# A four-layer attention and feed-forward kernel: the last layer's weights quantised in the second attention's last group, and its rows scaled on ScalarE

## The chip, the core and the metric

The kernel runs on one core of one Trainium2 chip. Such a core has TensorE (PE: matrix products and transposes by a product with the identity, with results in PSUM), VectorE (DVE), ScalarE (ACT), GpSimd (POOL) and SyncE (SP, which here only issues transfers). Each engine runs its own instruction stream; they meet through semaphores. The metric is the device time of one execution in microseconds, median of three runs.

## The reference, cut to what matters

```python
x = x + L0_xattn(layernorm(x), ctx)      # 16 heads of 64
x = x + L0_ffn(layernorm(x))             # top 2 of 8 experts
x = x + L1_xattn(layernorm(x), ctx)      # 16 heads of 16
x = x + L1_ffn(layernorm(x))

def quantize_w8_per(w, axis):            # per row or column
    amax = clip(max(abs(w), axis=axis, keepdims=True), 1e-08, None)
    scale = 127.0 / amax
    return clip(round(w * scale), -128.0, 127.0) / scale
def quantize_a16(x):                     # one scale for the whole tensor
    amax = clip(max(abs(x)), 1e-08, None)
    scale = 32767.0 / amax
    return clip(round(x * scale), -32768.0, 32767.0) / scale
def L1_ffn(x, W_in, b_in, W_out, b_out):
    hidden = gelu(quantize_a16(x) @ quantize_w8_per(W_in, axis=0) + b_in)
    return quantize_a16(hidden) @ quantize_w8_per(W_out, axis=1) + b_out
```

x is 8 batches of 512 rows of 256, W_in is 256x1024, W_out 1024x256, all float32. Because the activations have one scale, nothing of x can be quantised before the largest normalised value of all eight batches is known, and nothing of hidden before the largest of all hidden values.

## The kernel before, in words

The four layers run one after another, each in blocks in which every engine has its own stream and at whose end all engines meet. A batch is 512 rows, as QT = 4 tiles of 128 rows on the partitions. x stays in SBUF as `x_sb` from the experts to the end of the second attention and is also stored, batch by batch, to `x_between` in HBM, from which the last layer loads it.

**The second attention** (`second_attention`, L1200) goes through 8 batches of four groups of four heads. While PE and ScalarE work on the scores and exponentials of one group (`scores` L1498, `exps` L1657, `probs_v` L1505), PE computes the maximum scores of the next group and VectorE reduces them (`take_max`, L1754). In the very last group there is no next group, so VectorE's `attend` (L1776 and around) only keeps and divides the output of the group before (`keep_o` L1769, `divide`), and then waits for the last `keep_o`. After that come the transposes of the outputs (L1592), the output projection (L1612), the addition to x (L1826) and the store of the batch (L1411). On SP's queue the load of the input weights, `spare<-in_winT` (L1409), stands ahead of that store, as soon as `spare`, which the attention uses for its normalised rows, is free.

**The last layer** (`quantised_layer`, L1892) has five blocks; the change touches the first and the third.

1. Normalisation. SP loads the eight batches of x (`f_hid<-x_between`, L2012 for batches 0 and 1, each with its own semaphore, L2015 for 2 to 7, with one semaphore between them), two biases, and, when PE has turned the input weights and left `spare`, the output weights into `spare` (L2021). VectorE first quantises the input weights (`quantise_weights`, L1903: the largest magnitude of each row, 127 over it, eight scalings by row tile with a rounding constant added, one subtraction of it). PE turns them (L2031) and ScalarE copies them to `win`. Then for each batch VectorE takes the statistics (`row_statistics`: four `bn_stats` L67, four `bn_aggr` L73, variance plus epsilon L76), GpSimd raises that to the power -0.5 (L2095), VectorE subtracts the mean and multiplies (`scale_rows`, L84: four tiles) and reduces the largest magnitude (L2070), PE turns the batch (L2042: eight transposes) and ScalarE copies it to `xnT` (L2053). The statistics run one batch ahead; batches 2 to 6 are in a loop of two batches.
2. `whole_amax`: the maximum over partitions, through PE (L1962 to L1978).
3. First projection. For each batch VectorE rounds the rows (L2122), ScalarE makes the high part (L2177), VectorE the low part (L2128), PE multiplies both by `win` (L2168: 32 products), ScalarE applies gelu (L2183) and VectorE reduces the largest magnitude (L2135). After the first two batches' low parts VectorE quantises the output weights from `spare` into `wout` (the same L1903 to L1923).
4. `whole_amax` again, and 5. the second projection (L2252 to L2349) with the residual from `x_between`, the bias on GpSimd (L2332) and the store.

The order of every engine's work is written out by hand; there is no planner.

Of the kernel before, what the change touches and what calls it, by code (L numbers as in the profile page):

```python
# [13 lines left out]
P = 128  # L14
# [1185 lines left out]
def second_attention(nc, x_sb, ident, ident_r, mhalf, d, ctx_parts, x_dram, spare, s_win, s_xs):  # L1200


    with ExitStack() as ctx:
# [152 lines left out]
        def _(sp):  # L1356
# [38 lines left out]
            def batch(b, left):  # L1395
# [343 lines left out]
        def _(dve):  # L1739
# [59 lines left out]

            def keep_v(b, t):  # L1800
# [91 lines left out]
def quantised_layer(nc, ident, ones, mhalf, d, x_dram, out, spare, s_win, s_xs):  # L1892
# [5 lines left out]
    with ExitStack() as ctx:  # L1898
# [3 lines left out]
        def quantise_weights(dve, w, whole, top, s, inv, loaded, need, s_wq):  # L1902


            dve.wait_ge(loaded, need)
            nc.vector.tensor_reduce(top[:], w[:], AX.X, ALU.max, apply_absolute_value=True
                                    ).then_inc(s_wq, 1)
            dve.wait_ge(s_wq, 1)
            nc.vector.tensor_scalar(top[:], top[:], TINY, None, ALU.max).then_inc(s_wq, 1)
            dve.wait_ge(s_wq, 2)  # L1910
            nc.vector.reciprocal(s[:], top[:]).then_inc(s_wq, 1)
            dve.wait_ge(s_wq, 3)
            nc.vector.tensor_scalar(s[:], s[:], 127.0, None, ALU.mult).then_inc(s_wq, 1)
            dve.wait_ge(s_wq, 4)
            nc.vector.reciprocal(inv[:], s[:]).then_inc(s_wq, 1)

            for t in range(FFT):
                nc.vector.tensor_scalar(w[:, t, :], w[:, t, :], s[:, t:t + 1], MAGIC,
                                        ALU.mult, ALU.add).then_inc(s_wq, 1)
            flat = w[:].rearrange("p t k -> p (t k)")  # L1920
            whole = whole[:].rearrange("p t k -> p (t k)")
            dve.wait_ge(s_wq, 13)
            nc.vector.tensor_scalar(whole, flat, MAGIC, None, ALU.subtract).then_inc(s_wq, 1)  # L1923

# [7 lines left out]
        wout = sb("wout", [P, FFT, D], F32R)  # L1932
        bin_ = sb("b_in", [P, FFT])
        bout = sb("b_out", [P, D])
        win_max = sb("win_max", [P, FFT])
        win_s = sb("win_s", [P, FFT])
# [43 lines left out]
        with ExitStack() as ab:  # L1980
# [4 lines left out]
            with ExitStack() as a:  # L1985
# [20 lines left out]
                with nc.Block() as block:  # L2006
# [49 lines left out]
                    def _(dve):  # L2056
# [393 lines left out]
```

## Time and profile before

| | us |
|---|---|
| median of 3 runs (3283.21 to 3284.38) | 3283.84 |
| the profiled execution | 3282.52 |
| its span | 3280.7 |
| PE busy | 3100.5 (95%) |
| VectorE busy | 2288.7 (70%) |
| ScalarE busy | 1630.7 (50%) |
| GpSimd busy | 1304.9 (40%) |

The span is what the profile's records cover; some 1.8 us of the profiled execution lie around it. Times in the rows below count from its start. Busy shares are averages over the whole run; the last layer starts near 3058.9 and has other limits than the attentions that fill the rest. [...]

### The profile page before, as it was taken

How to read it: one execution, taken by the hardware profiler on the slowest of the kernel's cores; microseconds unless marked ns; L12 is line 12 of the kernel's file. 1: busy time of each engine (PE TensorE's matmuls, PEld its weight loads, DVE VectorE, ACT ScalarE, POOL GpSimd, SP SyncE). 2: the span in 40 equal slices, each digit the busy share in tenths (PEclk: the TensorE clock that was granted, in tenths of full speed). 3: DMA queues.
4: the chain of work that ended last, by engine and by line, in shares of the span. 5: the costliest groups of instructions: out<-in, count | busy, mean ns of one | idle time of the engine just before them, and what ended most of it. 6: DMA issues, size and time to landing. Idle time of an engine off the chain costs nothing. (4 is left out here: it accounts for less than half of the span.)

```text
span 3280.7 us, 40332 instructions
## 1 busy us (share of the span) xinstructions
PE 3100.5 (95%) x14204; PEld 1883.9 (57%) x14204; DVE 2288.7 (70%) x3680; ACT 1630.7 (50%) x1850; POOL 1304.9 (40%) x610
## 2 busy tenths in 40 slices
PE   6999999999999999999999969799999999999588
PEld 4556556556566565565565446455555555554368
DVE  5775775665766757757747434788888888888589
ACT  3453443443444434534534412376576666666388
POOL 1774774764765756747647723200000000000102
PEclk8999999999999999999999989799999999999698
DMA  8444553463453444444435232322323223322202
GB/s 233 113 117 120 127 139 90 117 158 85 117 145 90 119 125 118 107 122 113 120 100 124 65 113 73 83 49 64 71 49 69 66 49 72 67 50 57 72 13 90
DMA packets 182474, 317.40 MB, mean 97 GB/s; under 512 B 35080, under 2 KB 94288, under 8 KB 182288
## 3 DMA queue, kind: packets, MB, share of 16 engines
q1 hardware_dynamic: 182288, 315.00, 38.6%
q8 instruction: 107, 1.75, 0.2%
q14 instruction: 79, 0.65, 0.1%
HBM read 92.58 MB, written 29.36 MB: 37 GB/s over the span
## 5 line engine op out<-in xcount | busy, mean ns | idle before, releaser
L907 POOL TENSOR_TENSOR a_prob_sum<-a_prob_sum,a_prob 128x1024 f32<-128x1024 f32 x384 | 918.3, 2391 | 57.1 <-ACT a_prob L623 1.8
L623 ACT ACTIVATE a_prob<-a_t 128x1024 f32<-128x1024 f32 x512 | 517.0, 1025 | 647.9 <-PE a_t L442 461.9
L770 DVE TENSOR_REDUCE a_mhalves<-a_m 128x1 f32<-128x512 f32 x1024 | 688.6, 680 | 106.9 <-PE a_m L406 98.4
L1657 ACT ACTIVATE a_prob<-a_t 128x1024 f32<-128x1024 f32 x512 | 497.4, 1025 | 183.4 <-PE a_t L1498 182.7
L1754 DVE TENSOR_REDUCE a_mhalves<-a_m 128x1 f32<-128x512 f32 x807 | 537.2, 685 | 61.5 <-PE a_m L1477 57.5
L449 PE MATMUL a_o<-a_prob,a_v_all 128*64 128x512 f32 x2048 | 493.7, 604 | 0.0
L406 PE MATMUL a_m<-a_kh_n,a_qz 128*128 128x512 f32 x1024 | 416.9, 419 | 10.3 <-DVE a_kl_n L764 5.8
L907 POOL TENSOR_TENSOR a_prob_sum<-a_prob 128x1024 f32<-128x1024 f32 x64 | 153.5, 2398 | 557.5 <-ACT a_prob L623 494.3
L1477 PE MATMUL a_m<-a_vh,a_qz 128*128 128x512 f32 x807 | 337.1, 438 | 10.2 <-DVE x_sb L1826 4.4
L434 PE MATMUL a_t<-a_q_hl,a_k_hh 128*128 128x512 f32 x1024 | 325.1, 398 | 0.3 <-ACT a_prob L623 0.3
L442 PE MATMUL a_t<-a_q_hm,a_k_lm 66*128 66x512 f32 x1024 | 320.9, 394 | 0.0
L1498 PE MATMUL a_t<-a_qs,a_vs 128*128 128x512 f32 x1024 | 318.6, 400 | 1.6 <-ACT a_qs L1676 0.9
L406 PEld LDWEIGHTS a_m<-a_kh_n,a_qz 128*128 128x128 f32 x1024 | 187.4, 188 | 205.0 <-issue 95.7
L1868 POOL TENSOR_TENSOR a_rstd<-a_veps,mhalf 128x4 f32<-128x4 f32 x8 | 8.1, 1018 | 718.1 <-DVE a_veps L76 718.1
L786 DVE RECIPROCAL a_recip<-a_x 128x128 f32<-128x128 f32 x256 | 239.3, 944 | 48.5 <-PE a_x L465 48.5
L1505 PE MATMUL a_o<-a_prob,a_v_all 128*18 128x512 f32 x2048 | 269.7, 598 | 0.4 <-ACT a_prob L1657 0.4
L1477 PEld LDWEIGHTS a_m<-a_vh,a_qz 128*128 128x128 f32 x807 | 152.5, 190 | 191.4 <-DVE a_mhalves L1754 127.7
L449 PEld LDWEIGHTS a_o<-a_prob,a_v_all 128*64 128x64 f32 x2048 | 125.0, 136 | 223.7 <-issue 193.5
L761 DVE TENSOR_TENSOR a_ql_n<-a_x,a_qz 64x512 fp32r<-64x512 f32 x128 | 88.1, 689 | 227.4 <-ACT a_qz L639 225.2
L442 PEld LDWEIGHTS a_t<-a_q_hm,a_k_lm 66*128 66x128 f32 x1024 | 193.4, 189 | 43.5
L1498 PEld LDWEIGHTS a_t<-a_qs,a_vs 128*128 128x128 f32 x1024 | 184.9, 188 | 58.1 <-ACT a_prob L1657 17.1
L434 PEld LDWEIGHTS a_t<-a_q_hl,a_k_hh 128*128 128x128 f32 x1024 | 188.3, 189 | 50.3 <-ACT a_prob L623 11.1
(273 smaller groups left out, 4187.2 us busy)
## 6 DMA issues: line engine op xcount, KB each, us to landing
a_k_hh<-a_kh_n SPq DMA_DIRECT2D x256, 256.0 KB, 4.2
a_k_lm<-a_kl_n SPq DMA_DIRECT2D x128, 256.0 KB, 4.8
a_q_hl<-a_qz SPq DMA_DIRECT2D x128, 128.0 KB, 2.3
a_q_hm<-a_qz SPq DMA_DIRECT2D x128, 128.0 KB, 2.4
a_q_hl<-a_ql_n SPq DMA_DIRECT2D x128, 128.0 KB, 2.3
a_vs<-a_vh SPq DMA_DIRECT2D x256, 64.0 KB, 2.4
a_wq<-wq_parts SPq DMA_DIRECT2D x63, 256.0 KB, 2.6
a_wk<-wk_parts SPq DMA_DIRECT2D x63, 256.0 KB, 2.9
```

The source lines that it names most:

```text
L406: pe.matmul(ps_m[:, n, :], qz[:, hd, qt * P:(qt + 1) * P], kh_n[:, n * 512:(n + 1) * 512], start=True, stop=True).then_inc(s_mx, 1)
L434: pe.matmul(ps_t[t % 2][:, hd, :], k_hh[:, u, hd, keys], q_hl[:, u, hd, :], start=True, stop=False)
L442: mm = pe.matmul(ps_t[t % 2][:, hd, :], k_lm[0:HD0 + 2, u, hd, keys], q_hm[0:HD0 + 2, u, hd, :], start=False, stop=True)
L449: mm = pe.matmul(ps_o[hd * HD0:(hd + 1) * HD0, :], v_all[:, t, (2 * pr.p + hd) * HD0:(2 * pr.p + hd + 1) * HD0], prob[:, t % RING, hd, :], ...
L623: nc.scalar.activation(prob[:, t % RING], ps_t[t % 2][:, :, :], ACT.Exp, scale=SCALE0).then_inc(s_exp, 1)
L770: nc.vector.tensor_reduce(mhalves[:, qt, hd, n:n + 1], ps_m[:, n, :], AX.X, ALU.max).then_inc(s_max, 1)
L907: nc.gpsimd.tensor_tensor(acc, prob[:, (t - 1) % RING] if t == 1 else acc, prob[:, t % RING], ALU.add).then_inc(s_acc, 1)
L1477: pe.matmul(out, qz[:, u, h, qt * P:(qt + 1) * P], vh[:, G // 2 % 2, k * 512:(k + 1) * 512], start=True, stop=True).then_inc(s_mx, 1)
L1498: mm = pe.matmul(ps_t[j][:, h, :], vs[:, u, 2 * j + h, keys], qs[:, u, 2 * j + h, :], start=True, stop=True)
L1505: mm = pe.matmul(ps_o[QD * h:QD * h + VW, :], v_all[:, t, GH * n + h, :], prob[:, t % RB, h, :], start=(t == 0), stop=(t == KT - 1))
L1657: nc.scalar.activation(prob[:, t % RB, 2 * j:2 * j + 2, :], ps_t[j][:, :, :], ACT.Exp, scale=SCALE1).then_inc(s_exp, 1)
L1754: nc.vector.tensor_reduce(mhalfs[:, u, qt, h, k:k + 1], bank, AX.X, ALU.max).then_inc(s_max, 1)
```

## The change

- The output weights get their own tile `wout` and a half-size tile `raw`, allocated ahead of the experts. SP loads the input weights as before, then the first half of the output weights into `raw`, waits until VectorE has quantised it, and loads the second half; only then comes the wait and store of the last batch.
- In the second attention's last group VectorE, after `divide`, quantises the first half, the input weights, and the second half (`quantise_weights`, now a function of its own, for a range of row tiles). Both calls in the last layer are gone, and so is the load of the output weights there.
- In the normalisation block rows are scaled on ScalarE: rstd times x plus a shift, where the shift, minus the mean times rstd, is one VectorE operation of 128x4 for a batch. VectorE's order for a batch is now statistics two batches ahead, the largest magnitude, the shift two batches ahead. ScalarE scales batch b+1 before it copies batch b.
- All loops of that block are written out. GpSimd waits until ScalarE has read the rstd that it overwrites.

```diff
+def quantise_weights(nc, dve, w, whole, top, s, inv, tiles, done, before):
+    cols = slice(tiles[0], tiles[-1] + 1)
+    top, s, inv = top[:, cols], s[:, cols], inv[:, cols]
+    nc.vector.tensor_reduce(top, w, AX.X, ALU.max, apply_absolute_value=True).then_inc(done, 1)
+    dve.wait_ge(done, before + 1)
+    nc.vector.tensor_scalar(top, top, TINY, None, ALU.max).then_inc(done, 1)
+    dve.wait_ge(done, before + 2)
+    nc.vector.reciprocal(s, top).then_inc(done, 1)
+    dve.wait_ge(done, before + 3)
+    nc.vector.tensor_scalar(s, s, 127.0, None, ALU.mult).then_inc(done, 1)
+    dve.wait_ge(done, before + 4)
+    nc.vector.reciprocal(inv, s).then_inc(done, 1)
+    for t in range(len(tiles)):
+        nc.vector.tensor_scalar(w[:, t, :], w[:, t, :], s[:, t:t + 1], MAGIC,
+                                ALU.mult, ALU.add).then_inc(done, 1)
+    dve.wait_ge(done, before + 5 + len(tiles))
+    nc.vector.tensor_scalar(whole.rearrange("p t k -> p (t k)"), w.rearrange("p t k -> p (t k)"), MAGIC, None,
+                            ALU.subtract).then_inc(done, 1)
...
                     sp.wait_ge(s_kq, 3 * 2 * B)
-                    sp.dma_start(spare[:], d["winT"].rearrange("(t p) k -> p t k", p=P)).then_inc(s_win, 16)
+                    sp.dma_start(spare[:], d["winT"].rearrange("(t p) k -> p t k", p=P)).then_inc(last.s_win, 16)
+                    halves = d["wout2"].rearrange("(h t p) n -> h p t n", h=2, p=P)
+                    sp.dma_start(last.raw[:], halves[0]).then_inc(last.s_wout, 16)
+                    sp.wait_ge(last.s_woutq, 6 + FFT // 2)
+                    sp.dma_start(last.raw[:], halves[1]).then_inc(last.s_wout, 16)
...
+                    dve.wait_ge(last.s_wout, 16)
+                    quantise_weights(nc, dve, last.raw[:], last.wout[:, 0:FFT // 2, :], last.wout_max, last.wout_s,
+                                     last.wout_inv, range(FFT // 2), last.s_woutq, 0)
+                    dve.wait_ge(last.s_win, 16)
+                    quantise_weights(nc, dve, spare[:], spare[:], last.win_max, last.win_s, last.win_inv,
+                                     range(FFT), last.s_winq, 0)
+                    dve.wait_ge(last.s_wout, 32)
+                    quantise_weights(nc, dve, last.raw[:], last.wout[:, FFT // 2:, :], last.wout_max, last.wout_s,
+                                     last.wout_inv, range(FFT // 2, FFT), last.s_woutq, 6 + FFT // 2)
...
@@ -2014,86 +2044,95 @@
                             sp.dma_start(xt[:, b * QT:(b + 1) * QT], x_view[:, b * QT:(b + 1) * QT, :]
                                          ).then_inc(s_xl[2], 16)
-                        sp.dma_start(bin_[:], d["b_in"]).then_inc(s_wout, 16)
-                        sp.dma_start(bout[:], d["b_out2"]).then_inc(s_wout, 16)
-                        sp.wait_ge(s_wt, 2)
-                        sp.dma_start(spare[:], d["wout2"].rearrange("(t p) n -> p t n", p=P)).then_inc(s_wout, 16)
-                        sp.wait_ge(s_wout, 48)
+                        sp.dma_start(bin_[:], d["b_in"]).then_inc(s_bias, 16)
+                        sp.dma_start(bout[:], d["b_out2"]).then_inc(s_bias, 16)
+                        sp.wait_ge(s_bias, 32)
...
                             mm.then_inc(s_wt, 1)
-                        with pe.Fori(0, B // 2) as i:
-                            for u in range(2):
-                                b = 2 * i + u
-                                pe.wait_ge(s_xn, QT * (b + 1))
+                        for b in range(B):
+                            pe.wait_ge(s_xn, QT * (b + 1))
+                            if b:
                                 pe.wait_ge(s_xnT, b)
-                                for c in range(DCH):
-                                    for qt in range(QT):
-                                        mm = pe.transpose(ps_tr[:, c, qt * P:(qt + 1) * P],
-                                                          xn[:, u, qt, c * P:(c + 1) * P], ident[:])
-                                mm.then_inc(s_tr, 1)
+                            for c in range(DCH):
+                                for qt in range(QT):
+                                    mm = pe.transpose(ps_tr[:, c, qt * P:(qt + 1) * P],
+                                                      xn[:, b % 2, qt, c * P:(c + 1) * P], ident[:])
+                            mm.then_inc(s_tr, 1)
                     @block.scalar
                     def _(act):
                         for r in range(2):
                             act.wait_ge(s_wt, r + 1)
                             nc.scalar.copy(win[:, :, r * 512:(r + 1) * 512], ps_w[:]).then_inc(s_wk, 1)
-                        with act.Fori(0, B) as b:
+                        def scale(b):
+                            act.wait_ge(s_shift, b + 1)
+                            if b >= 2:
+                                act.wait_ge(s_tr, b - 1)
+                                act.wait_ge(s_xm, b - 1)
+                            for qt in range(QT):
+                                nc.scalar.activation(xn[:, b % 2, qt, :], xt[:, b * QT + qt, :], ACT.Identity,
+                                                     bias=shift[:, b % 2, qt:qt + 1],
+                                                     scale=rstd[:, b % 2, qt:qt + 1]).then_inc(s_xn, 1)
+                        scale(0)
+                        for b in range(B):
+                            if b + 1 < B:
+                                scale(b + 1)
                             act.wait_ge(s_tr, b + 1)
-                            nc.scalar.copy(xnT[:, :, bass.ds(b * NQ, NQ)], ps_tr[:]).then_inc(s_xnT, 1)
+                            nc.scalar.copy(xnT[:, :, b * NQ:(b + 1) * NQ], ps_tr[:]).then_inc(s_xnT, 1)
                     @block.vector
                     def _(dve):
-                        def rows_of(b):
-                            return [xt[:, bass.ds(b * QT + qt, 1), :].rearrange("p a f -> p (a f)")
-                                    for qt in range(QT)]
-                        def statistics(b, u):
-                            row_statistics(nc, dve, rows_of(b), stats[:, u], mv[:, u], veps[:, u, :], s_ln, 10 * b)
-                        def normalise(b, u):
-                            if not (isinstance(b, int) and b < 2):
-                                dve.wait_ge(s_tr, b - 1)
-                            scale_rows(nc, dve, rows_of(b), mv[:, u], rstd[:, u, :], xn[:, u], s_rstd, b + 1, s_xn)
+                        def statistics(b):
+                            if b < 3:
+                                dve.wait_ge(s_xl[b], 16 if b < 2 else 16 * (B - 2))
+                            u = b % 2
+                            row_statistics(nc, dve, [xt[:, b * QT + qt, :] for qt in range(QT)], stats[:, u], mv[:, u],
+                                           veps[:, u, :], s_ln, 10 * b)
+                        def shifts(b):
+                            dve.wait_ge(s_rstd, b + 1)
+                            nc.vector.scalar_tensor_tensor(shift[:, b % 2, :], mv[:, b % 2, :, 0], -1.0,
+                                                           rstd[:, b % 2, :], ALU.mult, ALU.mult
+                                                           ).then_inc(s_shift, 1)
+                        def largest(b):
                             dve.wait_ge(s_xn, QT * (b + 1))
-                            nc.vector.tensor_reduce(x_max[:, bass.ds(b, 1)], xn[:, u], AX.XY, ALU.max,
+                            nc.vector.tensor_reduce(x_max[:, b:b + 1], xn[:, b % 2], AX.XY, ALU.max,
                                                     apply_absolute_value=True).then_inc(s_xm, 1)
-                        quantise_weights(dve, spare, spare, win_max, win_s, win_inv, s_win, 16, s_wq)
-                        dve.wait_ge(s_xl[0], 16)
-                        statistics(0, 0)
-                        dve.wait_ge(s_xl[1], 16)
-                        statistics(1, 1)
-                        normalise(0, 0)
-                        dve.wait_ge(s_xl[2], 16 * (B - 2))
-                        with dve.Fori(0, B // 2 - 1) as i:
-                            statistics(2 * i + 2, 0)
-                            normalise(2 * i + 1, 1)
-                            statistics(2 * i + 3, 1)
-                            normalise(2 * i + 2, 0)
-                        normalise(B - 1, 1)
+                        statistics(0)
+                        statistics(1)
+                        shifts(0)
+                        shifts(1)
+                        for b in range(B):
+                            if b + 2 < B:
+                                statistics(b + 2)
+                            largest(b)
+                            if b + 2 < B:
+                                shifts(b + 2)
                     @block.gpsimd
                     def _(pool):
-                        with pool.Fori(0, B // 2) as i:
-                            for u in range(2):
-                                b = 2 * i + u
-                                pool.wait_ge(s_ln, 10 * b + 10)
-                                nc.gpsimd.tensor_tensor(rstd[:, u, :], veps[:, u, :], mhalf[:, 0:QT], ALU.pow
-                                                        ).then_inc(s_rstd, 1)
+                        for b in range(B):
+                            u = b % 2
+                            pool.wait_ge(s_ln, 10 * b + 10)
+                            if b >= 2:
+                                pool.wait_ge(s_xn, QT * (b - 1))
+                            nc.gpsimd.tensor_tensor(rstd[:, u, :], veps[:, u, :], mhalf[:, 0:QT], ALU.pow
+                                                    ).then_inc(s_rstd, 1)
             ps_a = psum("a", [P, 512], to=ab)
             ps_h = psum("h", [P, 4, NQ], to=ab)
...
@@ -2141,7 +2179,6 @@
                     low(0, 0)
                     rounded(1)
                     low(1, 1)
-                    quantise_weights(dve, spare, wout, wout_max, wout_s, wout_inv, s_mm, 1, s_wq2)
                     with dve.Fori(0, B // 2 - 1) as i:
```

## Rows read from the trace of the kernel before

**Rows 1.** Busy us by stretch and engine, PE's clock, DMA share, GB/s
```profile
core 0: us, PE busy (x) PEld busy (x) DVE busy (x) ACT busy (x) POOL busy (x), PEclk, DMA share, GB/s
3031.50:3050.77 19.27, 18.23 (x97) 6.05 (x98) 1.29 (x3) 16.22 (x17) 0.00 (x0) 1.00 0.00 1
...
3076.20:3109.48 33.28, 13.75 (x56) 10.98 (x56) 29.05 (x95) 7.08 (x7) 6.97 (x6) 0.50 0.06 18
```

**Rows 2.** Timeline of VectorE: start, us, engine, line, operation, idle before, releaser
```profile
3050.77 0.72 DVE L1769 STREAM_TRANSPOSE a_o_rows<-a_o 128x512 f32<-128x512 f32 x1 [17.92 <-PE a_o L1505]
```

**Rows 3.** Timeline of VectorE, the input weights quantised
```profile
3058.88 2.29 DVE L1906 TENSOR_REDUCE f_win_max<-spare 128x8 f32<-128x2048 f32 x1 [0.86 <-PEq L1203]
...
3061.96 2.14 DVE L1918 TENSOR_SCALAR spare<-spare,f_win_s 128x256 f32<-128x256 f32 x8
3064.14 1.23 DVE L1923 TENSOR_SCALAR spare<-spare 128x2048 f32<-128x2048 f32 x1
```

**Rows 4.** Timeline of VectorE, normalisation of the last layer
```profile
3076.22 1.40 DVE L67 BATCH_NORM_STATS2 f_stats<-f_hid 128x6 f32 x4 [4.45 <-DMA f_hid<-x_between]
...
3080.93 1.39 DVE L67 BATCH_NORM_STATS2 f_stats<-f_hid 128x6 f32 x4
...
3082.86 1.38 DVE L84 TENSOR_SCALAR f_xn<-f_hid,f_mv,f_rstd 128x256 f32 x4
3084.36 1.22 DVE L2070 TENSOR_REDUCE f_x_max<-f_xn 128x1024 f32 x1
3085.50 1.39 DVE L67 BATCH_NORM_STATS2 f_stats<-f_hid 128x6 f32 x4
```

**Rows 5.** Timeline of SP's queue, the two weight loads
```profile
3021.85 0.58 SPq L1409 DMA_DIRECT2D spare<-in_winT  x1
...
3070.55 0.42 SPq L2021 DMA_DIRECT2D spare<-in_wout  x1
```

**Rows 6.** DMA issues: count, KB each, us from issue to landing
```profile
spare<-in_winT SPq DMA_DIRECT2D x1, 1024.0 KB, 5.4
spare<-in_wout SPq DMA_DIRECT2D x1, 1024.0 KB, 8.7
```

**Rows 7.** Waits of PE, first projection block: us in total, times, longest
```profile
PE f_h L2168 <- ACT f_hid L2183: 7.1, 7, 1.2
PE f_h L2168 <- DVE f_x_low L2128: 4.8, 1, 4.8
```

**Rows 8.** Timeline of GpSimd, normalisation of the last layer
```profile
3078.32 1.07 POOL L2095 TENSOR_TENSOR f_rstd<-f_veps,mhalf 128x4 f32<-128x4 f32 x1 [7.77 <-DVE f_veps L76]
3083.02 1.25 POOL L2095 TENSOR_TENSOR f_rstd<-f_veps,mhalf 128x4 f32<-128x4 f32 x1 [3.64 <-DVE f_veps L76]
```

**Rows 9.** Groups by line on ScalarE: busy us, mean ns; then its timeline
```profile
L2310 ACT ACTIVATE f_h_high<-f_h_int,f_wout_inv 128x512 fp32r<-128x512 f32 x64 | 42.2, 707 | 0.0
...
L2183 ACT ACTIVATE f_hid<-f_h,f_b_in,f_h_scale 128x512 f32 x48 | 36.2, 781 | 6.0 <-PE f_h L2168 2.8
...
L1709 ACT CAST a_wv<-a_prob 128x256 fp32r<-128x256 f32 x1 | 0.4, 404 | 10.6 <-DMA a_prob<-in_v_w 10.6
...
3201.64 1.32 ACT L2310 ACTIVATE f_h_high<-f_h_int,f_wout_inv 128x512 fp32r<-128x512 f32 x2
```

**Rows 10.** Timelines of PE, ScalarE and VectorE, end of the normalisation block
```profile
3106.09 1.94 PE L2042 MATMUL f_tr<-ident,f_xn 128*128 128x128 f32 x8 [1.28 <-ACT f_xnT L2053]
...
3108.16 1.01 ACT L2053 COPY f_xnT<-f_tr 128x1024 f32 x1 [2.21 <-PE f_tr L2042]
...
3109.48 0.16 DVE L1962 TENSOR_REDUCE f_amax_x<-f_x_max 128x1 f32<-128x8 f32 x1 [2.81 <-PEq L2006]
```

**Rows 11.** Timeline, start of the second projection block
```profile
3194.16 3.54 DVE L2260 SCALAR_TENSOR_TENSOR f_h_low<-f_h_int,f_wout_inv,f_h_high 128x512 fp32r<-128x512 f32 x2 [0.88 <-ACT f_h_high L2310]
3194.38 5.56 POOL L2332 TENSOR_TENSOR f_xo<-f_xo,f_b_out 128x1024 f32<-128x1024 f32 x2 [91.55 <-DMA f_xo<-x_between]
...
3200.41 1.40 DVE L2260 SCALAR_TENSOR_TENSOR f_h_low<-f_h_int,f_wout_inv,f_h_high 128x512 fp32r<-128x512 f32 x2
```

More of the change, by code:

```diff
@@ L1197, in _, with __init__, sb, sem @@
             two_batches(B // 2 - 1, True)
-def second_attention(nc, x_sb, ident, ident_r, mhalf, d, ctx_parts, x_dram, spare, s_win, s_xs):
+class LastWeights:
+    def __init__(self, nc, ctx):
+        def sb(name, shape, dt=F32):
+            return ctx.enter_context(nc.sbuf_tensor("last_" + name, shape, dt))
+        def sem(name):
+            return ctx.enter_context(nc.semaphore("last_" + name))
+        self.wout = sb("wout", [P, FFT, D], F32R)
+        self.raw = sb("wout_raw", [P, FFT // 2, D])
+        self.win_max, self.win_s, self.win_inv = (sb("win_" + k, [P, FFT]) for k in ("max", "s", "inv"))
+        self.wout_max, self.wout_s, self.wout_inv = (sb("wout_" + k, [P, FFT]) for k in ("max", "s", "inv"))
+        self.s_win = sem("win_loaded")
+        self.s_wout = sem("wout_half_loaded")
+        self.s_winq = sem("win_steps")
+        self.s_woutq = sem("wout_steps")
+def quantise_weights(nc, dve, w, whole, top, s, inv, tiles, done, before):
[16 more added lines that the diff above has]
+                            ALU.subtract).then_inc(done, 1)
+def second_attention(nc, x_sb, ident, ident_r, mhalf, d, ctx_parts, x_dram, spare, last, s_xs):
     with ExitStack() as ctx:
@@ L1889, in _, with quantised_layer @@
                 add_bias(b)
-def quantised_layer(nc, ident, ones, mhalf, d, x_dram, out, spare, s_win, s_xs):
+def quantised_layer(nc, ident, ones, mhalf, d, x_dram, out, spare, last, s_xs):
     x_view = x_dram.rearrange("(t p) f -> p t f", p=P)
@@ L1900, in sb @@
             return to.enter_context(nc.sbuf_tensor("f_" + name, shape, dt))
[L1902 to L1923, printed above, removed]
         def psum(name, shape, to=ctx):
@@ L1992, in quantised_layer @@
                 rstd = sb("rstd", [P, 2, QT], to=a)
+                shift = sb("shift", [P, 2, QT], to=a)
                 ps_tr = psum("tr", [P, DCH, NQ], to=a)
                 ps_w = psum("w", [P, DCH, 512], to=a)
[L1995 to L1996 removed]
+                s_bias = sem("biases_loaded")
                 s_wt = sem("weights_transposed")
@@ L2026, in _ @@
                         for r in range(2):
-                            pe.wait_ge(s_wq, 14)
+                            pe.wait_ge(last.s_winq, 6 + FFT)
                             pe.wait_ge(s_wk, r)
@@ L2387, in build @@
         spare = sb("spare", [P, FFT, D])
-        s_win = ctx.enter_context(nc.semaphore("win_loaded"))
+        last = LastWeights(nc, ctx)
         s_xs = ctx.enter_context(nc.semaphore("x_between_stored"))
@@ L2392, in build @@
             experts(nc, x_sb, ident, mhalf, d, x_first)
-            second_attention(nc, x_sb, ident, ident_r, mhalf, d, ctx_parts, x_dram, spare, s_win, s_xs)
-        quantised_layer(nc, ident, ones, mhalf, d, x_dram, out, spare, s_win, s_xs)
+            second_attention(nc, x_sb, ident, ident_r, mhalf, d, ctx_parts, x_dram, spare, last, s_xs)
+        quantised_layer(nc, ident, ones, mhalf, d, x_dram, out, spare, last, s_xs)
 def layouts(x, ctx_768, L0_xattn_w_q, L0_xattn_w_kv, L0_xattn_w_out, L0_xattn_b_out,
```

12 lines of the change are left out of this document (2 added, 10 removed).

## The prediction

> **What bounds the kernel now.** I began with the page: its chain of waits only reaches back into the last layer's final block, so it says nothing about the stretch that the change touches. So I read busy time by stretch, then the timeline of one engine at a time, and then who waited for whom.
>
> [rows 1] cut the end of the run into stretches. From 3031.50 to 3050.77 (the second attention's last group) VectorE is busy 1.29 of 19.27 us, GpSimd not at all, while PE is busy 18.23.  From 3076.20 to 3109.48 VectorE is busy 29.05 of 33.28 us, PE 13.75, ScalarE 7.08: VectorE sets the pace of the last layer's normalisation. [rows 2] is the idle stretch seen from VectorE: 17.92 us before the transpose at 3050.77, so it was free from 3032.85.
>
> **1. The input weights, quantised earlier.** What goes from the start of the last layer is one reduction of 2.29 us, four small operations, eight scalings that take 2.14 in all, and a subtraction of 1.23 [rows 3]: from 3058.88 to 3065.37, 6.5 us (6.4 from start to start). It gives nothing there. The statistics of batch 2 wait for all six later row loads together, and those end the wait at 3076.22, after 4.45 us in which VectorE is idle already [rows 4]. The edit makes that idle time longer. The loads are issued behind the store of the last batch, and nothing here moves that store.
>
> Could the loads themselves end sooner? The 1 MB of output weights that went into the queue behind them at 3070.55 [rows 5] is gone from there. It landed 8.7 us after its issue [rows 6], at 3079.25, or 3.0 us after the rows: 1.05 MB in 3.0 us is 350 GB/s, the full rate, so it queued behind them and took nothing from them. I take 0; the other end is a saving of 3.0 us if it had shared the engines throughout, and below nothing there is no reason for a loss.
>
> Where the work goes: in the last group VectorE now does half of the output weights, the input weights, and the other half. From [rows 3] the whole of one matrix is 6.4 us from start to start, half of one is 1.15 + 0.8 + 1.1 + 0.6 = 3.6 us; together 3.6 + 6.4 + 3.6 = 13.6 us, in 17.92. From 3032.85 it ends at 3046.5, 4.3 us before the last transpose is due. Its transfers: the input weights are issued at 3021.85 [rows 5] and land 5.4 us later [rows 6], the first half directly behind them, so both are there by 3032.85. SP then waits for the first half's steps (about 3036.5) and loads the second half; even at the 5.4 us that the whole matrix took it lands at 3042, before VectorE wants it at 3042.9. Behind that wait on SP stands only the last batch's store, due some 20 us later; behind VectorE's waits stand the last transpose and all that follows. Cost 0, as long as the 4.3 us last.
>
> **2. The output weights, no longer quantised between the batches of the first projection.** Another 6.4 us of VectorE go. In that block PE waited for VectorE once, 4.8 us at its start, ahead of the quantisation; all its other waits there, 7.1 us in seven, were for ScalarE's gelus [rows 7]. VectorE had caught up by itself. I take 0. The ends: -0.5 us, a guess at one gelu's worth, and 0.
>
> **3. Rows scaled on ScalarE, batches unrolled.** This is the term that counts. In the old loop a batch costs VectorE 4.57 us, from 3080.93 to 3085.50 [rows 4]: statistics 1.93, four scalings to the reduction 1.50, reduction 1.14 to the next start. The new loop has statistics, reduction, and one 128x4 operation (the shift) that needs GpSimd's rstd. GpSimd starts 2.1 us after the statistics do and takes 1.07 or 1.25 [rows 8], mean 1.16; so the shift can start at 2.1 + 1.16 + 0.05 = 3.31 us. Statistics and reduction end their turn at 1.93 + 1.14 = 3.07, so VectorE waits 0.24 for GpSimd. With 0.08 until the next start the period is 3.39 us, against 4.57 and, on the alternate batches that carry the loop's branch, 4.71.
>
> From 3076.22 (call it 0): batch 2's statistics start at 0, batch 7's at 5 x 3.39 = 16.95. Its shift starts at 20.26, ends at 20.43, ScalarE starts at 20.53. One scaling of 128x256 with a scale and a bias from SBUF isn't in this trace. Bounds [rows 9]: a 128x256 cast takes 404 ns (four would take 1.3 us with their overlap); a gelu of 128x512 with both operands takes 781 (four: 3.1). Nearest by its operands: the 781 less 256 columns. A column costs (1012 - 404) / 768 = 0.8 ns by the copy of 1024 [rows 10] and the cast of 256, so 0.2 us go and 0.58 stay. Neighbours overlap by 0.1: two of f_h_high take 1.32 at 0.707 each. 3 x 0.48 + 0.58 = 2.0 us; it ends at 22.5. ScalarE then copies batch 6 (1.01), PE turns batch 7 (1.94, after 0.14), ScalarE copies it (1.01, after 0.12), and the next block's first reduction starts 0.3 later [rows 10]: 23.5, 25.6, 26.7, 27.0. Before, that reduction started at 3109.48, 33.26 after the same zero. Gain 33.26 - 27.0 = 6.2 us. The ends of ScalarE's term: 0.7 us more gain, or 1.1 less and further if it sets the period (rival B).
>
> Is the other ring slower? Copy, PE and copy again repeat every 1.01 + 0.14 + 1.94 + 0.12 = 3.21 us, and ScalarE's own work is 2.0 + 1.0 = 3.0: both under 3.39, barely. Batches 0 and 1 are scaled before 0 and only lend a margin. The reduction of batch 0 moves behind the zero; the first period of the new count holds it. More PE work per microsecond could raise its clock; in [rows 1] it stayed at 0.50 at 13.75 of 33.28 busy, and will be near 2 of 3.39.
>
> [...]
>
> **Sum.** 0 + 0 + 6.2 us. The profiled execution took 3282.52 us, so its like would take 3276.3. The median of the runs is 1.3 above the profiled one; 3283.84 - 6.2 = 3277.6.
>
> **Rivals.**
> - A, PE's clock rises. If the denser transposes bring full speed, the final 1.94 us halves at best, about 0.9 us: 3276.7. A warmer start of the next block, for which no row gives a price, I guess at up to 1 us more: 3275.7. For it: PE 58% busy instead of 41. Against it: [rows 1] show 0.50 throughout the old loop.
> - B, ScalarE and PE set the period. If a scaling takes 0.75 us (gelu's figure), ScalarE needs 3.0 + 1.0 = 4.0 us per batch: 0.6 x 5 + 1.0 = 4 us of the gain go, 3281.6. At 0.65 it is about 1.5 us, 3279.1. For it: the margin is only 0.15 to 0.4 us. Against it: the nearest row's arithmetic.
> - C, the straight code issues more slowly than the loops it replaces, by 0.2 to 0.5 us per batch: 1 to 3 us less gain, 3279 to 3280.6. Against it: in the old loop it is the batch with the branch that costs 0.14 more.
> - D, slower: the quantisation is stretched and the last group's end waits for it. VectorE operations do stretch here: two of f_h_low took 3.54 us at 3194.16 beside a GpSimd addition [rows 11]; later pairs take 1.40. At that factor, 2.5, the 13.6 us become 34, overrun the 17.92 by 16, and the kernel ends at 3277.6 + 16 = 3293.6. It costs from a stretch of 1.3 on and makes the kernel slower from 24.1 us, a stretch of 1.8. Against it: GpSimd is busy 0.00 in that stretch [rows 1]. [...]
> - E, the row loads end earlier without the output weights behind them: up to 3.0 us more gain, 3274.6.
>
> **Chances.** Forecast 0.62 (own range 3276.8 to 3278.4), A 0.15, B 0.12, C 0.04, D 0.04, E 0.03. 0.2% of the median is 6.6 us, about what a measurement of this kernel can tell from no change, and the forecast lies 0.4 short of it. So faster takes A, E and 0.28 of the forecast: 0.46. Same takes the other 0.34, B and C: 0.50. Slower is D: 0.04. The range from 3275.4 to 3280.4 leaves out D, E's far end and B's worse half.
>
> **What would show it.** Quantisation between 3033 and 3047, the last transpose still at 3050.8. VectorE idle about 10 us before batch 2's statistics, which start at 3076.2. A period of 3.4 us with a short wait for GpSimd; four scalings in 2.0 us; the first reduction of the next block at 3103.2. From there to the end the same 171 us. Wrong if the last transpose is late, if the period is near 4, or if the gap to the end changes by over 1 us.

## The result, and the profile after

The changed kernel takes 3275.77 us (median of 10 runs, 3271.84 to 3277.45); the kernel before, run beside it, 3284.95 us (10 runs, 3282.94 to 3286.82). The ratio is 0.9972, 95% interval 0.9963 to 0.9980: 9.2 us (0.28%) faster. The forecast was 3277.6 us, a gain of 6.2. In all that follows, medians and ratios leave out three executions that were slow (3869.07 and 8995.73 us of the kernel before, 8314.91 of two_banks_again).

The profiled execution after took 3271.84 us with a span of 3270.0, against 3282.52 and 3280.7 before. Its time by five marks, in us from mark to mark:

| | before | after | difference |
|---|---|---|---|
| start to the last transpose of the second attention | 3050.77 | 3049.24 | -1.53 |
| transpose to the issue of the last store of rows | 7.27 | 7.27 | 0 |
| store to the statistics of batch 2 | 18.18 | 17.25 | -0.93 |
| those statistics to the next block's first reduction | 33.26 | 25.86 | -7.40 |
| from there to the end | 171.22 | 170.38 | -0.84 |

The rows behind it, in the order of the run. VectorE's timeline in the last group (start, us, engine, line, operation, idle before and its releaser), where [rows 2] had 17.92 us of idle time:

```profile
3031.24 1.21 DVE L1225 TENSOR_REDUCE last_wout_max<-last_wout_raw 128x4 f32<-128x1024 f32 x1
...
3034.96 2.28 DVE L1225 TENSOR_REDUCE last_win_max<-spare 128x8 f32<-128x2048 f32 x1
...
3041.36 1.22 DVE L1225 TENSOR_REDUCE last_wout_max<-last_wout_raw 128x4 f32<-128x1024 f32 x1
...
3044.47 0.69 DVE L1239 TENSOR_SCALAR last_wout<-last_wout_raw 128x1024 fp32r<-128x1024 f32 x1
3049.24 0.72 DVE L1817 STREAM_TRANSPOSE a_o_rows<-a_o 128x512 f32<-128x512 f32 x1 [4.08 <-PE a_o L1553]
```

The three quantisations fill 3031.24 to 3045.16, 13.9 us, and the transpose still waits for PE at the end, by 4.08 us (13.6 and 4.3 were predicted). No wait for a transfer stands between them. SP's queue shows how the loads moved; the one at 3070.55 in [rows 5] is gone:

```profile
3019.78 0.58 SPq L1452 DMA_DIRECT2D spare<-in_winT  x1
3020.40 0.58 SPq L1454 DMA_DIRECT2D last_wout_raw<-in_wout  x1
3035.07 0.37 SPq L1457 DMA_DIRECT2D last_wout_raw<-in_wout  x1
3056.51 0.38 SPq L1459 DMA_DIRECT2D x_between<-x_sb  x1
```

VectorE in the normalisation, as in [rows 4]:

```profile
3073.76 1.41 DVE L67 BATCH_NORM_STATS2 f_stats<-f_hid 128x6 f32<-128x256 f32 x4 [5.21 <-DMA f_hid<-x_between]
...
3075.61 0.17 DVE L76 TENSOR_SCALAR f_veps<-f_mv 128x4 f32<-128x4 f32 x1
3075.69 1.21 DVE L2112 TENSOR_REDUCE f_x_max<-f_xn 128x1 f32<-128x1024 f32 x1
3076.90 0.16 DVE L2106 SCALAR_TENSOR_TENSOR f_shift<-f_mv,f_rstd 128x4 f32<-128x4 f32 x1
3076.98 1.40 DVE L67 BATCH_NORM_STATS2 f_stats<-f_hid 128x6 f32<-128x256 f32 x4
...
3099.62 0.16 DVE L1991 TENSOR_REDUCE f_amax_x<-f_x_max 128x1 f32<-128x8 f32 x1 [3.09 <-PEq L2036]
```

A batch now takes 3.22 us instead of 4.57 or 4.71, with no idle time in brackets: the shift starts as soon as the reduction ends. GpSimd, for [rows 8]:

```profile
3075.86 1.01 POOL L2134 TENSOR_TENSOR f_rstd<-f_veps,mhalf 128x4 f32<-128x4 f32 x1 [7.52 <-DVE f_veps L76]
3079.08 1.01 POOL L2134 TENSOR_TENSOR f_rstd<-f_veps,mhalf 128x4 f32<-128x4 f32 x1 [2.21 <-DVE f_veps L76]
```

The first of these ends at 3076.87, 0.03 us before the shift could start, and GpSimd is idle 2.21 us between batches. And ScalarE at the end of the block, for [rows 10]:

```profile
3093.21 2.07 ACT L2084 ACTIVATE f_xn<-f_hid,f_shift,f_rstd 128x256 f32<-128x256 f32 x4 [0.25 <-DVE f_shift L2106]
3095.19 0.99 ACT L2093 COPY f_xnT<-f_tr 128x1024 f32<-128x1024 f32 x1
3098.30 1.01 ACT L2093 COPY f_xnT<-f_tr 128x1024 f32<-128x1024 f32 x1 [2.12 <-PE f_tr L2067]
```

Four scalings take 2.07 us, and ScalarE waits 0.25 us for the shift: VectorE sets the pace, ScalarE nearly does. By stretch, columns as in [rows 1] (PEclk is PE's granted clock, 1.00 being full speed):

```profile
3031.24:3049.24 18.00, 17.10 (x95) 5.46 (x94) 13.41 (x35) 14.97 (x16) 0.00 (x0) 1.00 0.11 30
3073.76:3099.62 25.86, 12.63 (x53) 10.00 (x51) 21.28 (x74) 18.82 (x31) 6.04 (x6) 0.50 0.00 1
```

### The profile page after: what moved, and what is told of

It reads as the page before. It is cut to its first block and busy times, and to the rows that moved or that the text cites. A ratio compares the mean times of both kernels' runs of the same rounds, so it can differ in the third digit from the quotient of the medians.

```text
span 3270.0 us, 40220 instructions
## 1 busy us (share of the span) xinstructions
PE 3093.9 (95%) x14204; PEld 1877.8 (57%) x14204; DVE 2281.8 (70%) x3662; ACT 1645.7 (50%) x1882; POOL 1304.3 (40%) x610
## 5 line engine op out<-in xcount | busy, mean ns | idle before, releaser
L406 PE MATMUL a_m<-a_kh_n,a_qz 128*128 128x512 f32 x1024 | 415.3, 417 | 10.7 <-DVE a_kl_n L764 5.6
```

Source lines behind the costliest of these rows:

```text
L406: pe.matmul(ps_m[:, n, :], qz[:, hd, qt * P:(qt + 1) * P], kh_n[:, n * 512:(n + 1) * 512], start=True, stop=True).then_inc(s_mx, 1)
```

## Experiments

Most of the difference between two single traces lies in one place, but the start and the end differ too. The experiments ask which part of the change gives what, and which marks scatter without a cause in the code. The kernel before has one trace. The stretch that the change touches runs from the issue of the last store of rows (SP's queue) to the next block's first reduction (VectorE), and is read from each trace:

| kernel | store to batch 2's statistics | from there to the reduction | both | median less that of before, same chip |
|---|---|---|---|---|
| before | 18.18 | 33.26 | 51.44 | |
| after | 17.25 | 25.86 | 43.11 | -9.2 |
| after_again | 17.30 | 25.86 | 43.16 | -8.1 |
| weights_early_only | 18.39 | 33.27 | 51.66 | +0.1 |
| rows_scaled_only | 17.33 | 25.87 | 43.20 | -7.6 |
| unrolled_on_vector | 17.26 | 32.25 | 49.51 | -1.5 |
| vector_loop_only | 17.60 | 33.11 | 50.71 | +1.2 |
| last_group_filled | 17.33 | 25.86 | 43.19 | -0.6 |
| own_semaphores | 11.89 | 26.28 | 38.17 | -13.2 |
| own_semaphores_again | 11.95 | 26.29 | 38.24 | -13.8 |
| own_semaphores_weights_late | 12.38 | 28.43 | 40.81 | -10.6 |
| two_banks | 11.98 | 23.62 | 35.60 | -16.0 |
| two_banks_again | 11.92 | 23.63 | 35.55 | -16.9 |

What the fourth column lies under the 51.44 of before agrees with the last column to within some 1 us, except in vector_loop_only (1.9 apart) and in last_group_filled, whose added work lies outside this stretch.

**after_again**: the changed kernel once more, no edit.

> The changed kernel once more. Mine: the profile of it ends 10.7 us before that of the kernel before, of which 1.5 us lie ahead of the last group's final transpose and 0.8 behind the normalisation block; both are scatter between executions and come out anew (between -1.5 and +2 us), while from the last transpose to batch 2's statistics (24.5 us) and from there to the next block's first reduction (25.9 us) nothing moves by over 0.1. Rival, layout: the new tiles move every later tile in SBUF and give the 1.5 us; then the last transpose is again at 3049.2, within 0.3.

3276.26 us (11 runs, 3274.22 to 3277.86), ratio 0.9976 [0.9967, 0.9985]. The marks that the change touches come back to 0.05 us. The last transpose does not: 3052.29 here, 3049.24 in the first trace, and 3049.5 to 3053.7 in the other kernels without added work there, so its 1.53 us in the first pair were chance. The store was issued 8.95 us after it instead of 7.27; the two stretches from transpose to store, first of after, then of after_again:

```profile
3049.24:3056.51 7.27, 4.90 (x24) 3.66 (x24) 3.09 (x7) 1.01 (x1) 0.00 (x0) 1.00 0.00 0
```

```profile
3052.29:3061.24 8.95, 6.58 (x24) 4.80 (x24) 3.09 (x7) 1.01 (x1) 0.00 (x0) 0.81 0.00 0
```

The 24 matrix products take 6.58 us instead of 4.90, at a mean granted clock of 0.81 instead of 1.00, with the same work before them: the clock falls to 0.50 about 4 us after the transpose and is back at 1.00 3.4 us later. So 1.7 us come and go in this stretch between executions of one kernel. Over all twelve traces without added work in the last group it has two values, 7.27 us in four and 8.93 to 8.96 in eight; before and after happened to be profiled with the shorter one.

**weights_early_only**: the quantisations moved, the normalisation block as before (loops, VectorE scales).

```
-   for b in range(B): ...                     # after: unrolled, ScalarE scales
+   with pe.Fori(0, B // 2) as i: ...          # as before, on all four engines
+   with dve.Fori(0, B // 2 - 1) as i:
+       statistics(2 * i + 2, 0); normalise(2 * i + 1, 1) ...
```

> Weights quantised in the last group, normalisation block as before (rows scaled on VectorE, in loops). Mine: only the transfers gain: 24.5 us from the last transpose to batch 2's statistics instead of 25.4, then 33.3 us as before; about 0.9 us under the kernel before, plus what the two later blocks give (0 to 0.8). Rival, the weights are what pays: over 3 us under the kernel before.

3284.42 us (11 runs; before 3284.32), ratio 1.0002 [0.9993, 1.0011]. 13 us of work left VectorE's way in the last layer and the time stayed. VectorE's idle time grew instead: it waits 6.72 us for the load of batch 0 and 5.20 for batches 2 to 7, where before it had waited 4.45 for the latter alone. And the output weights' load, absent here, had delayed nothing: 18.39 us from store to statistics, against 18.18 with it.

**rows_scaled_only**: the complement; normalisation of after, weights loaded and quantised where they were.

```
-   quantise_weights(...)  x3 in the last group, and their loads
+   sp.dma_start(spare[:], d["wout2"]...)      # behind the row loads again
+   quantise_weights(... win ...)              # ahead of statistics(0)
+   quantise_weights(... wout ...)             # between low(1, 1) and the loop
```

> Rows scaled on ScalarE and unrolled; weights quantised and loaded where they were. Mine: 25.4 us to batch 2's statistics, 25.9 us from there to the next block, 7.4 us under the kernel before; and the first projection block takes 78.5 us with the quantisation in it, as before. Rival, the quantisation in the projection block costs once the rest is faster: that block is over 80 us.

3276.68 us (11 runs), ratio 0.9976 [0.9967, 0.9985]: the whole gain of after_again (3276.26 on the same chip) to 0.4 us, with none of the moved work. The first projection took 78.18 us with the quantisation in it, 78.13 and 76.98 us without it in the two traces of after. The two of after differ in PE's granted clock, which goes from 0.50 to 1.00 some 12.4 us into the block in the first (and at about 12 in before and in rows_scaled_only) and 9.9 us into it in the second; those 2.5 us at full instead of half speed are worth about the 1.2 us between them. At a like clock the quantisation costs 0.05 us here, and 0.35 in before (78.48).

**unrolled_on_vector**: after, with the rows scaled on VectorE again; everything stays unrolled. With the scaling VectorE's old order comes back too (statistics one batch ahead, no shift).

```
-   act: nc.scalar.activation(xn[...], xt[...], ACT.Identity, bias=shift, scale=rstd)
+   dve: scale_rows(nc, dve, [xt[:, b * QT + qt, :] for qt in range(QT)], ...)
```

> The changed kernel with the rows scaled on VectorE again, all loops still written out. It tells how much of the block's 7.4 us is the unrolling. Mine: VectorE's period falls from 4.57 and 4.71 to 4.49, so the block takes 32.4 us instead of 33.3 and ScalarE's scaling is worth the other 6.5; GpSimd's rstd is again 1.07 or 1.25 us, beside scalings on VectorE, where it is 1.01 without them. Rival, the loops were what cost: under 30 us. Rival for rstd, it is the loop and not VectorE's scaling: 1.01 here too.

3282.00 us (12 runs), before 3283.54, ratio 1.0002 [0.9985, 1.0020], an interval that one execution of 3315.84 us widens (the other eleven lie between 3278.32 and 3284.99). The medians alone could not tell; the trace can. The block takes 32.25 us, 1.01 less than with loops, and the statistics start 0.92 us sooner after the store. VectorE and GpSimd in one batch of it:

```profile
3086.22 0.17 DVE L76 TENSOR_SCALAR f_veps<-f_mv 128x4 f32<-128x4 f32 x1
3086.30 1.38 DVE L84 TENSOR_SCALAR f_xn<-f_hid,f_mv,f_rstd 128x256 f32<-128x256 f32 x4
3086.47 1.25 POOL L2116 TENSOR_TENSOR f_rstd<-f_veps,mhalf 128x4 f32<-128x4 f32 x1 [3.23 <-DVE f_veps L76]
```

The same 128x4 power takes 1.24 to 1.26 us beside VectorE's scalings, in every batch of the block, and 1.01 beside the reduction in after. So the rival for rstd fails; the 1.07 of every other batch appears only where VectorE runs its loop. Why the power takes longer beside the scalings, no run here shows.

**vector_loop_only**: unrolled_on_vector with only VectorE's loop put back.

```
-   for b in range(1, B): ...
+   with dve.Fori(0, B // 2 - 1) as i:
+       statistics(2 * i + 2, 0); normalise(2 * i + 1, 1)
+       statistics(2 * i + 3, 1); normalise(2 * i + 2, 0)
```

> unrolled_on_vector with VectorE's loop over the batches put back in the normalisation block; TensorE, ScalarE and GpSimd stay unrolled. Theory (VectorE's own loop carries the rest of what unrolling gave): the third batch's statistics start 18.2 to 18.4 us after the issue of the last store of rows instead of 17.3, and from there to the first maximum over the normalised rows takes 33.3 us instead of 32.3, as in the kernel before; the time is that of the kernel before within 1 us. Rival (the 0.9 us are the issue of the loads, or the other engines' loops): 17.3 us stays, and 32.3 us stays; the time lies 1.9 us under the kernel before.

3285.24 us (11 runs), before 3284.02, ratio 1.0002 [0.9993, 1.0010]. In the block the theory holds: 33.11 us, 0.86 of the 1.01. Ahead of it, it mostly fails: 17.60 us, only 0.34 of the 0.92. The other 0.6 us go with the loops of the other engines, or with something that differs along with them. The issue of the six row loads, in SP's queue, may be part of it; it is 0.3 us shorter here than before (first before, then here):

```profile
3061.96 6.43 SPq L2015 DMA_DIRECT2D f_hid<-x_between  x6
```

```profile
3065.49 6.13 SPq L2045 DMA_DIRECT2D f_hid<-x_between  x6
```

But in rows_scaled_only the same issue takes 5.75 us and the statistics start no sooner (17.33), so this isn't shown, and the 0.6 us stay open. The median, 1.9 us above what the marks say, is within the scatter of the stretches outside them.

**last_group_filled**: after, with 9.2 us more work for VectorE in the last group.

```
+   for k in range(4):
+       nc.vector.tensor_reduce(last.extra[:], spare[:], AX.X, ALU.max, ...)
```

> The changed kernel with four more reductions of 128x2048 on VectorE in the last group (9.2 us, results unused), to find the edge of the cover. Mine: the quantisation ends 4.1 us before the last transpose is due, so the transpose comes 5.1 us late, and the kernel takes 5.1 us more than the changed one. Rival, VectorE's work in that group already slows PE or ScalarE: more than 5.1, with the group's products or exponentials longer. Rival, the end of the group isn't on the path: 0.

3282.92 us (10 runs), before 3283.54: of the gain (8.1 or 9.2 us) only 0.6 is left. VectorE and PE around the end of the group:

```profile
3048.57 9.24 DVE L1863 TENSOR_REDUCE last_extra<-spare 128x8 f32<-128x2048 f32 x4
3057.72 0.71 DVE L1819 STREAM_TRANSPOSE a_o_rows<-a_o 128x512 f32<-128x512 f32 x1
```

```profile
3051.61 1.05 PE L1555 MATMUL a_o<-a_prob,a_v_all 128*18 128x512 f32 x8 [0.39 <-ACT a_prob L1707]
...
3059.23 0.69 PE L1642 MATMUL a_m<-ident,a_o_n 128*128 128x128 f32 x2 [5.76 <-DVE a_o_n L1826]
3061.02 2.07 PE L1662 MATMUL a_o<-a_wo,a_prob 128*128 128x256 f32 x4 [1.10 <-ACT a_prob L1753]
```

PE's context products end at 3052.66 and the transpose comes 5.06 us later: 9.24 of added work less the cover of 4.1. That much was expected, and as all of the cost. But PE then waits 5.76 us, and its next products run at the half clock (0.50 from 3056.9 to 3067.1): four of the output projection take 2.07 us, against 1.13 in the trace of before, and the store follows the transpose after 10.49 us instead of 7.27 or 8.95. So overrunning the cover cost 5.1 us and another 1.5 to 3.2. The clock falls in this stretch without the overrun too (after_again), so that the long wait makes the fall longer rests on this one trace. The rival's mechanism did not show: eight of the group's context products take 1.05 us as before.

**own_semaphores**: after, each batch of rows with a semaphore of its own, so that batch 2 doesn't wait for batch 7's load.

```
-   s_xl = [sem("x_loaded0"), sem("x_loaded1"), sem("x_loaded")]
+   s_xl = [sem(f"x_loaded{b}") for b in range(B)]
...
-   if b < 3:
-       dve.wait_ge(s_xl[b], 16 if b < 2 else 16 * (B - 2))
+   dve.wait_ge(s_xl[b], 16)
```

> The changed kernel with a semaphore for each batch's load, so that batch 2's statistics wait for batch 2 alone. Mine: they start near 3068.5 on the changed kernel's clock instead of 3073.8, and the ring of ScalarE's copy, PE's turn and the next copy, 3.2 us a batch from batch 0 on, sets the pace: 4.3 us under the changed kernel. Rival, the loads set the pace (1.5 us a batch) and VectorE gets all back: 5.2 us. Rival, VectorE's and ScalarE's reads slow the loads or are slowed by them: under 3 us.

3271.17 us (5 runs), 5.1 us under after_again on the same chip; ratio to before 0.9962 [0.9948, 0.9976]. The wait for all six loads was what held batch 2's statistics; they now start 11.89 us after the store. ScalarE and PE while they catch up:

```profile
3075.43 1.01 ACT L2090 COPY f_xnT<-f_tr 128x1024 f32<-128x1024 f32 x1
3076.33 2.08 ACT L2081 ACTIVATE f_xn<-f_hid,f_shift,f_rstd 128x256 f32<-128x256 f32 x4
3076.58 1.94 PE L2064 MATMUL f_tr<-ident,f_xn 128*128 128x128 f32 x8 [1.19 <-ACT f_xnT L2090]
3078.56 1.01 ACT L2090 COPY f_xnT<-f_tr 128x1024 f32<-128x1024 f32 x1
```

Copy, transposes, copy repeat every 3.13 us with PE waiting 1.19 for the copy, from batch 0 to batch 7: the second ring of the prediction (3.21). VectorE goes at 3.22 ahead of it and waits for no load from batch 1 on, and the ring ends the block. So the expected mechanism holds; it gave 4.9 us by the marks instead of 4.3.

**own_semaphores_weights_late**: the same on top of rows_scaled_only.

> A semaphore per load, rows scaled on ScalarE, but the weights loaded and quantised where the kernel before does it. With one wait for all loads this move was worth nothing. Mine: now the quantisation (6.4 us from the block's start) ends about when batch 0 lands, and the weights' turn on PE and copy on ScalarE fall between the first batches' turns and start the ring later: 2 to 3.5 us slower than with the weights early. Rival, still worth nothing: within 0.5 us. Rival, all 6.4 us come back.

3272.91 us (5 runs), 10.6 us under before; ratio 0.9968 [0.9955, 0.9980]. Store to reduction is 2.6 us longer than in own_semaphores. VectorE is only 0.5 us late at batch 2's statistics; the rest comes through ScalarE, whose first scaling stands behind its second copy of the turned weights:

```profile
3073.53 1.01 ACT L2060 CAST f_win<-f_w 128x1024 fp32r<-128x1024 f32 x1 [2.12 <-PE f_w L2043]
3074.44 4.04 ACT L2069 ACTIVATE f_xn<-f_hid,f_shift,f_rstd 128x256 f32<-128x256 f32 x8
```

That scaling starts 13.42 us after the store, against 10.78 in own_semaphores, and the ring of copies starts 2.6 us later. So the moved input weights pay as soon as the wait for all loads no longer hides this, as expected; in the change as it stands they don't.

**two_banks**: own_semaphores, and two sets of PSUM banks for the transposes, started tile by tile.

```
-   ps_tr = psum("tr", [P, DCH, NQ], to=a)
+   ps_tr = psum("tr", [P, 2, DCH, NQ], to=a)
...
-   pe.wait_ge(s_xn, QT * (b + 1))
-   if b: pe.wait_ge(s_xnT, b)
+   if b >= 2: pe.wait_ge(s_xnT, b - 1)
+   for qt in range(QT):
+       pe.wait_ge(s_xn, QT * b + qt + 1)
```

> The kernel with a semaphore per load, and in addition two sets of PSUM banks for the turned rows, PE turning each tile of rows as soon as it is scaled. In the kernel without them ScalarE's copies follow each other every 3.13 us, which is copy, PE's turn and copy. Mine: with two sets VectorE's 3.22 us a batch is the pace, the ring's 0.4 us goes and the tail after the last shift shortens by 2.1 us: the block ends 2.5 us earlier. Rival, PE's clock rises with the denser work and gives more. Rival, single tiles cost PE its overlap of loads and products: no gain.

3267.58 us (5 runs, 3265.08 to 3269.83), ratio 0.9949 [0.9937, 0.9962]. PE and ScalarE at its end:

```profile
3092.30 2.08 ACT L2081 ACTIVATE f_xn<-f_hid,f_shift,f_rstd 128x256 f32<-128x256 f32 x4 [0.24 <-DVE f_shift L2102]
3093.05 2.07 PE L2064 MATMUL f_tr<-ident,f_xn 128*128 128x128 f32 x8 [1.14 <-ACT f_xn L2081]
3094.28 1.90 ACT L2090 COPY f_xnT<-f_tr 128x1024 f32<-128x1024 f32 x2
3096.49 0.16 DVE L1991 TENSOR_REDUCE f_amax_x<-f_x_max 128x1 f32<-128x8 f32 x1 [0.86 <-PEq L2036]
```

The last transposes start 0.75 us after the scaling starts and end 0.7 us after it ends; in after they began only 1.0 us after its end, behind the copy. The block shrinks by 2.66 us; the period, VectorE's, stays 3.22. PE's granted clock does rise here, to 1.00 for 3.4 us around batch 2's transposes (in own_semaphores it is 0.50 throughout the block), but it is 0.50 again from batch 3 on, so the end of the block, which gives the gain, runs at the old clock.

**own_semaphores_again** and **two_banks_again**: both on one further chip, since the first two ran on different ones.

> own_semaphores once more, on one chip with two_banks_again. Theory: its gain over the changed kernel is one of structure (5.1 us then), so it comes back on another chip: 11.5 to 14 us under the kernel before. Rival (a good part was scatter between chips): under 10 us below the kernel before.

> two_banks once more beside own_semaphores_again: the pair on one chip. Theory: a second set of PSUM banks takes TensorE's turn out of the ring of ScalarE's copies: 2.5 to 3.6 us under own_semaphores_again, some 15 to 17 us under the kernel before. Rival (the two chips made the difference of 3.6 us): under 1.5 us between them.

3270.24 us (5 runs), ratio 0.9958 [0.9945, 0.9971], and 3267.09 us (5 runs), ratio 0.9948 [0.9935, 0.9961]; before 3284.02. The gains of structure hold on another chip, 13.8 and 16.9 us, and the pair on one chip is 3.2 us apart (2.7 by the marks). Both kernels beat the changed one, by 4.9 and 7.6 us from store to reduction.

## Why the prediction was right, step by step

**The time**: within the stated range (3275.4 to 3280.4), but 0.4 us from its edge and below the forecast's own 3276.8 to 3278.4. It is nearest to the time of rival A (3275.7), which did not happen, and that is chance. The gain was 9.2 us against 6.2: 1.2 of the missing 3.0 lie in the block, 0.9 ahead of it, and the rest, some 0.9, is scatter of the medians. On whether a change would be told from none the prediction leaned the other way: it gave "same" 0.50 and "faster" 0.46, and the interval of the ratio ends at the 0.2% that it had set.

**What bounds the kernel there**: right. VectorE set the pace of the normalisation before and does after. That the chain of waits ends too late to say so held as well.

**1, the input weights moved, worth 0**: right, by weights_early_only and rows_scaled_only, two sides of one cut. The cover held as worked out (4.08 us left of 4.3), and the loads arrived in time. The reason given, that the statistics wait for all six loads, is shown by own_semaphores: without that wait 5 us go, and the moved weights are worth 2.6. Between the last store and batch 2's statistics VectorE of after waits 13.1 us in all (6.83, 1.05 and 5.21), not about 10, and the longest wait is for batch 0's load. Rival E, loads that end earlier without the output weights behind them, is refuted: the kernel that drops that load and keeps the loops has 18.39 us, the one that keeps it, unrolled, has 17.33. The 350 GB/s that the prediction calls the full rate is what the row loads reach alone: 348 to 352 GB/s from 3066 to 3072 in the trace of after, where no output weights follow them, and 348 to 353 from 3066 to 3074 in that of before. That no load here could go faster is not shown: the row loads reach 373 from 3062 to 3064 in after.

**2, the output weights, worth 0**: right to what can be read: 0.05 to 0.35 us between traces with a like clock, within the 0 to 0.5 that the prediction allowed, while the two traces of after differ by 1.2.

**3, rows on ScalarE, worth 6.2**: right in mechanism, short in size; the block gave 7.40. The mis-sized term is GpSimd's power. It was taken as the mean of 1.07 and 1.25, with VectorE waiting 0.24 us for it in each batch and a period of 3.39. Both durations had been read beside VectorE's scalings, which the change takes away: it takes 1.01, the wait is gone, and the period is 3.22, VectorE's own work. The block was to take 27.0 us and took 25.86. Of these 1.14 us the five periods make 0.84 (batch 7's statistics start at 16.11 instead of 16.95), the shift 0.17 (it starts 3.14 behind them, not 3.31), and the tail 0.13 (6.61 from the shift's start to the reduction, where 6.74 had been worked out). The scaling was sized well: 2.07 us for four against 2.0.

**What the prediction left out**: what unrolling gives ahead of the block, 0.9 us; its term for that stretch was 0. In the block 1.01 of the 7.40 us come from unrolling and 6.39 from the move to ScalarE (unrolled_on_vector); there the prediction lost nothing by it, since it built the new period from its parts. It named only the 0.14 of the alternate batches and treated straight code as a risk (rival C, whose 0.2 to 0.5 us per batch no row shows), which did not happen. 7.4 + 0.9 = 8.3 us is the gain of structure, against 9.2 and 8.1 in the medians; the 10.7 us between the two profiled executions hold another 2.4 that are chance.

**The other rivals**: A did not happen (eight transposes of 128x128 do take 1.06 us at a clock of 1.00, L2058 of after, against 1.97 at 0.50, L2031 of before): the granted clock in the block is 0.50 after as before, and in the first projection it rises to 1.00 about 12 us after the reduction in both traces. In after_again it rises 2.5 us sooner, but so it does in unrolled_on_vector, whose transposes are hardly denser than before, so this is no gain of the change. B came near: ScalarE waits 0.25 us per batch for VectorE, the margin that was worked out. D did not happen: three quantisations took 13.9 us with GpSimd idle. But its price past the cover was too low: last_group_filled shows 1.5 to 3.2 us of PE's clock added to it.

## What to carry to other kernels

When an engine that sets the pace waits for a transfer at one place, work taken out ahead of that wait is worth nothing until the wait itself is cut (here 0, and 2.6 us once it was); look first at a semaphore that several loads share. Read the duration of a helper's operation beside the neighbour that it will have after the change, not the one it has before (here 1.01 against 1.07 to 1.26 us). To price a change of a few us, compare marks on both sides of the touched stretch in several traces, since the stretches around it scatter by as much (here 1.7 us in one of them).

## What the runs showed of the hardware

- GpSimd's power of 128x4 took 1.01 us beside VectorE's reduction and 1.07 to 1.26 beside its scalings of 128x256, the latter in four kernels (before, weights_early_only, unrolled_on_vector, vector_loop_only).
- TensorE's granted clock in the output projection fell to 0.50 for a while in eight of twelve executions, with no cause found in the code (mean 0.81 over 8.95 us, against 1.00 over 7.27). After a wait of 5.76 us the mean was 0.55 over 10.49 us, in the one trace that has such a wait:

```profile
3057.72:3068.21 10.49, 7.39 (x18) 5.30 (x18) 3.09 (x8) 1.01 (x1) 0.00 (x0) 0.55 0.00 0
```

- Loops over the batches on four engines went with 1.0 us more in the block and 0.9 us more ahead of it; VectorE's loop alone accounts for 0.86 and 0.34 of these. What the rest ahead of the block is stays open.
- Where TensorE's clock rose to 1.00 in the first projection (about 10 or 12 us into it) went with a difference of 1.2 us in that block between two executions of one kernel (76.98 and 78.13 us).
